# State-space stage of a two-layer decoder: 64 of the 128 rows of each response matrix are loaded, the two halves of a sequence become two stationary blocks, and two channels share the TensorE array in two row halves

## The reference

```
x1     = x @ w1_w.T + w1_b
x_conv = silu(depthwise_conv(x1, conv_w))         # 3 taps along the sequence
x_ssm  = ssm(x_conv, A, B_ssm, C_ssm, D_ssm)
v      = silu(x @ v1_w.T + v1_b)
return x_ssm * v @ w2_w.T + w2_b

def step(h, xt):                                  # ssm: a scan along the sequence
    h = h * Abar + xt[..., None] * B_ssm          # Abar = sigmoid(A), 16 states a channel
    y = jnp.einsum('bcs,cs->bc', h, C_ssm) + D_ssm * xt
    return (h, y)
```

## Time and profile before

| what | value |
|---|---|
| median of three runs | 1748.66 us (1745.78 to 1757.88) |
| the profiled execution | 1752.65 us, span 1750.8 us |
| mean granted TensorE clock | 0.907 |
| PE busy | 1431.1 us (82%), 10593 matmul records |
| DVE, ACT, POOL busy | 900.4, 510.0, 489.2 us |
| DMA | 337.5 MB, 193 GB/s over the span |

### The profile page before, as it was taken

The page is one execution under the profiler, slowest core; times in us unless marked ns, Lnnn a source line. Parts: engine busy times, 40 slices in busy tenths (PEclk is TensorE's granted clock), DMA queues, the critical chain, the costliest instruction groups (busy, mean ns, idle before and its releaser), DMA issues. The chain is left out here.

```text
span 1750.8 us, 29233 instructions
## 1 busy us (share of the span) xinstructions
PE 1431.1 (82%) x10593; PEld 1088.6 (62%) x10593; DVE 900.4 (51%) x2499; ACT 510.0 (29%) x1312; POOL 489.2 (28%) x481
## 2 busy tenths in 40 slices
PE   7666888659999997459999689988985467999978
PEld 4454666549999996235566355555554245888867
DVE  6354566551111112997772354767675534555534
ACT  3202232212222221001111144445554212555520
POOL 1011000011111102523322010135355624665544
PEclk9797999869999998678999899999996668999989
DMA  7674877759989981899994000001012596444456
GB/s 213 185 242 141 326 308 304 282 196 364 329 326 328 328 322 58 206 253 253 252 250 97 27 13 1 13 31 55 31 64 97 207 361 206 149 151 147 149 217 232
DMA packets 171303, 337.50 MB, mean 193 GB/s; under 512 B 11936, under 2 KB 134448, under 8 KB 165648
## 3 DMA queue, kind: packets, MB, share of 16 engines
q1 hardware_dynamic: 151808, 285.73, 50.8%
q0 software_dynamic: 15888, 43.52, 7.0%
q10 hardware_dynamic: 3456, 6.29, 1.1%
HBM read 182.90 MB, written 152.60 MB: 192 GB/s over the span
## 5 line engine op out<-in xcount | busy, mean ns | idle before, releaser
L153 PE MATMUL bank<-arena 128*128 128x128 f32 (+7 forms) x10593 | 1431.1, 332 | 313.7 <-DVE arena L153 219.2
L153 PEld LDWEIGHTS bank<-arena 128*128 128x128 f32 (+5 forms) x10593 | 1088.6, 176 | 655.8 <-issue 274.2
L153 ACT ACTIVATE arena<-bank 128x512 f32<-128x512 f32 (+3 forms) x627 | 269.3, 466 | 861.5 <-PE bank L153 807.9
L153 POOL TENSOR_TENSOR arena<-arena 128x512 f32<-128x512 f32 (+4 forms) x140 | 149.2, 1066 | 730.7 <-DVE arena L153 606.9
L153 ACT ACTIVATE arena<-bank,arena 128x256 f32<-128x256 f32 (+3 forms) x478 | 202.0, 459 | 252.8 <-PE bank L153 171.1
L153 DVE TENSOR_TENSOR arena<-bank,arena 128x128 f32<-128x128 f32 (+5 forms) x331 | 123.7, 388 | 175.5 <-PE bank L153 94.4
L153 DVE TENSOR_SCALAR arena<-bank,arena 128x128 f32<-128x128 f32 (+2 forms) x196 | 66.1, 393 | 247.3 <-PE bank L153 243.0
L153 POOL DMA_INDIRECT ys<-arena x146 | 153.1, 1049 | 133.7 <-ACT arena L153 72.0
L153 DVE COPY arena<-bank 128x256 f32<-128x256 f32 (+2 forms) x136 | 76.9, 578 | 132.2 <-PE bank L153 123.5
L153 DVE TENSOR_REDUCE arena<-bank 128x4 f32<-128x512 f32 (+1 forms) x128 | 81.1, 684 | 66.2 <-PE bank L153 62.6
L153 DVE TENSOR_SCALAR arena<-arena 128x256 f32<-128x256 f32 (+10 forms) x286 | 91.2, 349 | 44.2 <-POOL arena L153 30.3
(11 more groups left out here) (22 smaller groups left out, 169.5 us busy)
## 6 DMA issues: line engine op xcount, KB each, us to landing
arena<-in_bank SPq DMA_DIRECT2D x41, 2052.0 KB
xs<-arena SPq DMA_DIRECT2D x32, 2193.0 KB, 26.3
xsa<-arena SPq DMA_DIRECT2D x16, 2193.0 KB, 11.4
arena<-kd SPq DMA_DIRECT2D x16, 1024.0 KB, 8.6
arena<-xs SPq DMA_DIRECT2D x114, 129.0 KB
arena<-ys SPq DMA_DIRECT2D x16, 896.0 KB, 5.6
arena<-in_bank SPq DMA_DIRECT2D x8, 1536.0 KB, 9.6
arena<-in_banka ACTq DMA_DIRECT2D x24, 256.0 KB
```

The source lines that it names most:

```text
L153: ins = fn(*a, **kw)
```

## The change

The lower half of the rows of a response tile repeats the upper half, shifted by 64 columns. The new kernel loads only the 64 rows that begin at offset 64, and gives partitions 0 to 63 to a channel of the first 128 and partitions 64 to 127 to a channel of the second 128: a tile then holds 32 channels, there are eight tiles, and each is filled by two transfers of 64 partitions. A channel's filter is now two matmuls into the same place: the first half of the sequence (64 x 32 stationary) with all 128 columns, and the second half with the first 64 columns, accumulated on the last 64 output columns. The two channel blocks write two banks. Phase A lays the two halves of the sequence side by side in `xcT`, so its step 4 uses matmuls with the identity as the moving operand and 64 columns of data stationary instead of transposes, and it waits for both SiLUs.

```diff
+            for m in range(2):
+                src = bass.AP(tensor=kd.tensor, offset=(128 * m + 16 * q) * 256 + 64, ap=[[1, 64], [256, 16], [1, 128]])
+                got.append(S.dma(s.dma_start, view(tb, 0, [[128, 16], [1, 128]], 64 * m, 64 * m + 64), src, lanes[(2 * q + m) % 10], w=[h_kd, *tw]))
...
-            for m, y2, h in ys:
-                bk, bw = ps.get()
-                T.wait(h, *bw)
+            got = [ps.get() for _ in range(2)]
+            T.wait(*[h for _, _, h in ys], *got[0][1], *got[1][1])
+            for half, (bk, _) in enumerate(got):
                 for b in range(4):
-                    h = tr(bank(bk)[:, b * 128:(b + 1) * 128], y2[:, b * 128:(b + 1) * 128], ident, sig=(b == 3))
+                    for m, y2, _ in ys:
+                        at = b * 128 + 64 - 64 * half
+                        h = mm(bank(bk)[64 * m:64 * m + 64, b * 128:(b + 1) * 128], y2[:, at:at + 64], ident, True, True, sig=(b == 3 and m == 1))
+                h_xc[g] = V(v.tensor_copy, view(xcT, 16 * half + 4 * g, [[1, 4], [32, 128]]), view(bank(bk), 0, [[128, 4], [1, 128]]), w=[h], free=True)
...
-            for c in range(16):
-                i, j = c // 4, c % 4
-                h = mm(bank(bk)[32 * j:32 * j + 32, i * 128:(i + 1) * 128], xcT[:, (q * 16 + c) * 16:(q * 16 + c) * 16 + 32], tb[:, c * 128:(c + 1) * 128],
-                       True, True, sig=(c == 15))
+            for i in range(4):
+                for half in range(2):
+                    for j in range(4):
+                        c = 4 * i + j
+                        at = (q * 16 + c) * 32 + 16 * half
+                        for m in range(2):
+                            r64 = slice(64 * m, 64 * m + 64)
+                            h = mm(bank(got[m][0])[32 * j:32 * j + 32, i * 128 + 64 * half:(i + 1) * 128], xcT[r64, at:at + 32],
+                                   tb[r64, c * 128:(c + 1) * 128 - 64 * half], half == 0, half == 1, sig=(c == 15 and half == 1 and m == 1))
...
-            if q + 5 < 16:
+            if q + 5 < 8:
...
-            h = A(a.activation, u, bank(bk), ACT.Copy, w=[h, *uw])
-            ps.put(bk, h)
-            yield
+            for m in range(2):
+                u, uw = turned.get()
+                hu = A(a.activation, u, bank(got[m][0]), ACT.Copy, w=[h, *uw])
+                ps.put(got[m][0], hu)
+                us.append((u, hu))
+            yield
+            for m, (u, h) in enumerate(us):
+                bk, bw = ps.get()
+                T.wait(h, *bw)
+                for i in range(4):
+                    h = tr(bank(bk)[:, i * 128:(i + 1) * 128], u[:, i * 128:(i + 1) * 128], ident, sig=(i == 3))
...
-        pipeline([state_space(q) for q in range(16)])
+        pipeline([state_space(q) for q in range(8)])
```

More of the change, by code:

```diff
@@ L374, in build @@
         h_vt, h_xc = {}, {}
-        lanes = [Lane(sem()) for _ in range(5)]
+        lanes = [Lane(sem()) for _ in range(10)]
         def load_toeplitz(q):
             tb, tw = mP.get()
-            src = bass.AP(tensor=kd.tensor, offset=q * 16 * 256, ap=[[1, 128], [256, 16], [1, 128]])
-            return tb, S.dma(s.dma_start, view(tb, 0, [[128, 16], [1, 128]]), src, lanes[q % 5], w=[h_kd, *tw])
+            got = []
+            for m in range(2):
+                src = bass.AP(tensor=kd.tensor, offset=(128 * m + 16 * q) * 256 + 64, ap=[[1, 64], [256, 16], [1, 128]])
+                got.append(S.dma(s.dma_start, view(tb, 0, [[128, 16], [1, 128]], 64 * m, 64 * m + 64), src, lanes[(2 * q + m) % 10], w=[h_kd, *tw]))
+            return tb, got
         toeplitz = deque(load_toeplitz(q) for q in range(5))
@@ L426, in phase_a @@
             yield
-            for m, y2, h in ys:
-                bk, bw = ps.get()
-                T.wait(h, *bw)
+            got = [ps.get() for _ in range(2)]
+            T.wait(*[h for _, _, h in ys], *got[0][1], *got[1][1])
+            for half, (bk, _) in enumerate(got):
                 for b in range(4):
-                    h = tr(bank(bk)[:, b * 128:(b + 1) * 128], y2[:, b * 128:(b + 1) * 128], ident, sig=(b == 3))
+                    for m, y2, _ in ys:
+                        at = b * 128 + 64 - 64 * half
+                        h = mm(bank(bk)[64 * m:64 * m + 64, b * 128:(b + 1) * 128], y2[:, at:at + 64], ident, True, True, sig=(b == 3 and m == 1))
+                h_xc[g] = V(v.tensor_copy, view(xcT, 16 * half + 4 * g, [[1, 4], [32, 128]]), view(bank(bk), 0, [[128, 4], [1, 128]]), w=[h], free=True)
+                ps.put(bk, h_xc[g])
+            for m, y2, _ in ys:
                 cy.put(y2, h)
-                h_xc[g] = V(v.tensor_copy, view(xcT, m * 2048 + 4 * g, [[1, 4], [16, 128]]), view(bank(bk), 0, [[128, 4], [1, 128]]), w=[h], free=True)
-                ps.put(bk, h_xc[g])
             yield
@@ L444, in state_space @@
         def state_space(q):
-            bk, bw = ps.get()
+            got = [ps.get() for _ in range(2)]
             tb, h = toeplitz.popleft()
-            T.wait(h, *bw)
-            for c in range(16):
-                i, j = c // 4, c % 4
-                h = mm(bank(bk)[32 * j:32 * j + 32, i * 128:(i + 1) * 128], xcT[:, (q * 16 + c) * 16:(q * 16 + c) * 16 + 32], tb[:, c * 128:(c + 1) * 128],
-                       True, True, sig=(c == 15))
+            T.wait(*h, *got[0][1], *got[1][1])
@@ L453, in state_space @@
             mP.put(tb, h)
-            if q + 5 < 16:
+            if q + 5 < 8:
                 toeplitz.append(load_toeplitz(q + 5))
-            u, uw = turned.get()
-            h = A(a.activation, u, bank(bk), ACT.Copy, w=[h, *uw])
-            ps.put(bk, h)
-            yield
[L460 to L464, removed]
@@ L465, in state_space @@
-            h = V(v.tensor_copy, view(ssm, q * 16, [[4, 4], [1, 4], [256, 16]]), view(bank(bk), 0, [[128, 4], [32, 4], [1, 16]]), w=[h], free=True)
-            ps.put(bk, h)
-            ssm_h.append(h)
+            us = []
+            for m in range(2):
[3 more added lines that the diff above has]
+                us.append((u, hu))
+            yield
+            for m, (u, h) in enumerate(us):
[3 more added lines that the diff above has]
+                    h = tr(bank(bk)[:, i * 128:(i + 1) * 128], u[:, i * 128:(i + 1) * 128], ident, sig=(i == 3))
+                turned.put(u, h)
+                h = V(v.tensor_copy, view(ssm, 128 * m + q * 16, [[4, 4], [1, 4], [256, 16]]), view(bank(bk), 0, [[128, 4], [32, 4], [1, 16]]), w=[h], free=True)
+                ps.put(bk, h)
+                ssm_h.append(h)
```

## The result

The changed kernel takes 1761.39 us (median of 20 runs, 1752.79 to 1770.5) against 1750.51 (20 runs, 1742.21 to 1762.03) for the kernel before: a ratio of 1.0061, 95% interval 1.0041 to 1.0082. It is 10.9 us slower where 11.6 less were forecast. The profiled execution took 1753.06 us, span 1751.3, clock 0.904; it is one of the quickest, so that the profile shows less loss than the median.

What follows compares the result with a forecast made beforehand. Loads and the PE-ACT ring were taken to bound the stage, loads being slower at the upper clock. Phase B at 92.9 instead of 104.52, 11.6 us less, took the median 1748.66 to 1737; range 1729 to 1752.

Steps and rivals of the forecast that it cites:

- Issue could also hold it ... I take 1.32: Channel matmuls: 128 records a step take 1.32 us at the upper clock, with starts about 0.007 us apart.
- Nothing waits for them earlier: Later weights: issued at about 74 instead of 93.97, with nothing waiting for them before the barrier.
- Half-tile loads at zero: Response tile loads in the stage: three remaining tiles stay hidden behind the cycles, counted as zero time.
- Phase A: Step 4 before the stage: costs 3.5 us more, moving the first channel matmul from 56.12 to 59.7.
- The ring: Cycle of transposes, matmuls and ACT copies: 3.36 us at the upper clock, 5.43 at the lower.
- The clock: PE clock in the stage: low at first, rises after two cycles and stays up.
- All that follows the barrier shifts as one block: Stages after the barrier: all move by the same amount, a plain shift.
- Issue as the bound: Rival, channel matmuls: 0.026 us a record, a step 3.3 us, time 1749; chance 0.20 together with half overlap.
- Tiles that exclude each other: Rival, channel matmuls: only two of eight small tiles run at a time, a step 5.3 us, time 1769; chance 0.07.
- The floor of 25 ns between starts: Skill's limit on matmul starts: a step would need 3.2 us, time near 1748; counted under the issue rival.

Runs made afterwards that it cites:

- e7: The changed kernel with 13 small matmuls added ahead of the barrier and nothing else; ratio 1.0048 to the kernel before.
- e8: The kernel before with each channel matmul cut into two of 64 columns, same loads; ratio 1.0020 to the kernel before.
- e2: The changed kernel with all eight tiles loaded ahead and the later weights held until the last channel matmuls are done; ratio 1.0005 to the kernel before.
- e9: The changed kernel with all tiles ahead, weights held and 13 small matmuls added ahead of the barrier, a repeat on another chip; ratio 0.9980 to the kernel before.
- e6: The kernel before with 50 small matmuls added ahead of the barrier; ratio 1.0014 to the kernel before.
- e10: The changed kernel with all tiles ahead, weights held and 45 small matmuls added ahead of the barrier; ratio 0.9981 to the kernel before.
- e5: The changed kernel with all tiles ahead, weights held and 13 small matmuls added ahead of the barrier; ratio 0.9958 to the kernel before.
- e4: The kernel before with ten whole response tiles loaded ahead instead of five and the later weights held; ratio 0.9981 to the kernel before.

## Why the prediction was wrong

**The step that failed** is "Issue could also hold it ... I take 1.32". It asked how far apart two starts can be, took 0.007 us from four starts after a wait, and was nearly right on that: bursts of 128 records take 1.88 us here and 2.90 at the lower clock (e7, forecast 1.6 and 2.9). It did not ask whether 272 instructions a step can be delivered. In the stage 10.6 us of pauses stand in the first profile and 13.4 in the second, and phase B starts at 107.92 and 113.74, not 92.9. e8 shows that a larger count makes pauses without any other part of the change; e2 against the changed kernel shows that without transfers beside the stage the loss is not there.

The lists of transfers in the traces tie the two together. Ten profiles have such pauses in this stage, 33 in all, and every one of them ends 2.3 to 3.0 us after the start of a block on q8. What differs is how long after the end of a pause the next block starts: 4.2 to 6.6 us in 14 of 17 cases beside half-tiles or weights (about 1.1 in the other three, each the last pause of its stage), 2.5 to 3.9 in the three of e8 beside whole tiles, and 1.0 to 3.4 in 13 cases with next to nothing else moving. So a block starts late beside those loads, and PE waits for it. Why it sometimes takes 3 us with nothing else moving, and sometimes 1, is open.

**"Nothing waits for them earlier"** failed with it. The weights were issued from 71.70 (forecast 74) and nothing waited for them, but transfers ran at 347 GB/s beside the fetch of instructions; with the weights held back the later pauses are gone, and the ratio is 1.0036 in place of 1.0072 (the intervals overlap). A transfer that is moved has a price for what is fetched beside it, even if nobody waits for it.

**Half-tile loads at zero** was right on waits (PE never waited for a tile), but took a load that nobody waits for to cost nothing. A half-tile of 512 KB lands after 7.1 us, a whole one of 1024 KB after 7.3; the rate from 28 on is 190 to 253 GB/s, against 273 to 365 before. So the three tiles that are loaded in the stage are under way for longer beside the fetch of instructions. (The Trainium skill, "DMA: Bandwidth & Descriptors", section "Rules for kernel authors", advises one transfer of 128 partitions over two to disjoint halves; the trace agrees, with these numbers.)

**Phase A** was right: step 4 of the last group takes 58.74 - 54.27 = 4.47 us to the first channel matmul (4.7 forecast), which starts at 58.74, 59.68 and 60.10 in three profiles (59.7 forecast). **The ring** was sized too small: 3.67 measured, 3.36 forecast, some 2 us over the stage. **The clock** rose at 57 in the first profile, before the first cycle (two cold ones were forecast), but was lost again: 0.89 on average from 58.74 to 74.30, 0.60 to 91.10, 0.79 to the end, and between 71 and 102 bursts, some of them only parts of a step, take 3.7 to 4.8 us in place of 2.96. The forecast had let it stay, since it saw no pause.

**"All that follows the barrier shifts as one block"** failed in the profile: the shift grows by 5.0 and 8.0 us between 166 and 395, with 2.5 and 2.7 us of pauses, and moving the edges takes most of it away (2.1 in e7, 1.0 in e9) or brings it to the kernel before (7.9 in e6). What it costs in the time is open: e7 and e10 don't resolve it, and in e2 the shift grows by 8.4 us with a ratio of 1.0005.

**The rivals.** Issue as the bound was nearest in its cause, at 1749, with the right place and the wrong size: it was priced at 0.026 us a record, where the instructions come a block at a time, and the price depends on what else is being transferred. Tiles that exclude each other: nearer in number, at 1769, but refuted by 1.88 us a burst, where 5.3 were named. The floor of 25 ns between starts (the Trainium skill, "TensorE: Matmul & The Clock Gate", Part 1) would make 127 x 0.025 = 3.2 us of it, as an estimate; the trace has 1.88 for matmuls in different parts of the array.

**What is left of the change.** With all tiles ahead and the weights held back, the changed form runs at 1.0005 of the time before (e2), and with 13 or 45 small matmuls more at 0.9958, 0.9980 and 0.9981 (e5, e9, e10); the old form with ten ahead at 0.9981 (e4). Only the intervals of e5 and e4 stay below 1. The old form has that gain from earlier loads alone, and no run shows that the new matmuls add to it.

## What to carry to other kernels

Cutting a matmul into smaller ones that run side by side saves array time but multiplies instructions, and these are a stream of transfers themselves: here 16 KB for some 256 instructions, a block every 3.7 us in steps without a pause (e5) and every 8.4 beside half-tiles and weights. So count instructions per microsecond of a new burst, not only the pace between two, look for pauses of PE with no releaser, and keep bulk loads away from such a burst. And a load that nobody waits for isn't free to be moved forward.

## What the hardware showed

Eight matmuls of 64 x 32 in two row halves and four column groups run together: 128 records in 1.88 us, 0.015 each. Two transfers into 64 partitions each move some 215 GB/s where one into 128 moves some 300 to 350. And the place in the program at which a block of instructions ends can be seen in a later stage: 52 instructions that do nothing useful took the pauses between 165 and 395 from 3.2 us (e2) to none (e5).
